# Value projections in quarters, a third slot of lag, and weights laid out before the launch

## The chip, the cores and the metric

The kernel runs on one core of a Trainium2 chip. The metric is the device time of the whole program in microseconds, the median of several runs. The engines are TensorE (PE; its weight loads are listed as PEld), VectorE (DVE), ScalarE (ACT), GpSimd (POOL) and SyncE (SP), which issues most DMAs. They run their own instruction streams in order and wait for one another on semaphores.

## What is computed

One decoder layer for 16 sequences of 128 tokens with 256 features, with layer norms in front of its three parts:

```python
x = x + attn(layernorm(x))            # 16 heads of 64, fixed-point rounding
x = x + xattn(layernorm(x), ctx)      # ctx: (16, 128, 128), 16 heads of 64
x = x + ffn(layernorm(x))             # d_ff 1024, two of 8 experts by LoRA of rank 16

# attn
q, k, v = make_fxp(x @ w_qkv.T)       # clip to +-8, truncate to 1/4096
dots = make_fxp(q @ k.T * 64 ** -0.5)
attn = make_fxp(softmax(dots))
out = make_fxp(attn @ v)
out = make_fxp(out @ w_proj.T + b_proj)

# xattn: the same without make_fxp; k and v from ctx
# ffn: sum over 2 experts of top_v[k] * relu(h @ wi.T + (h @ A.T) @ B.T) @ wo.T
```

All tensors are float32. The kernel reaches that precision on TensorE with operands split into a high part (type F32R) and a low part: every large product is three matmuls, low x high, high x low, high x high (`split3`, lines 405 to 407).

## The kernel before

The 16 sequences form G = 4 groups of 4, 512 tokens each. The kernel runs self-attention for the four groups, then cross-attention for the four, then the feed-forward for the four. The functions of these stages are named a_, b_ and c_. The x tile stays in SBUF throughout.

In an attention stage a group has eight slots, one for each pair of heads. A slot s of self-attention issues on TensorE, in this order (`a_slot`, line 505): the q block and the k block of pair s (6 matmuls of 512 columns each, `a_block`); the transposes of the softmax weights of slot s-2 (`a_transpose`); the output projection of slot s-3 (`project_out`, 12 matmuls of 256 columns); the product of weights and values of slot s-2 (`a_attend`); in slots 0 to 3 alone, two value blocks of 512 columns, each for one sequence and half of the heads; and the scores of slot s (`a_scores`). The lag of two slots gives the softmax time: ScalarE takes signs (the rounding to fixed point needs them) and exponentials, VectorE converts to int16 and clips, and takes the reciprocal of the sums, GpSimd multiplies the exponentials by it (`a_weights`, tile p_int). There is one buffer each of e_sb, p_int and rsum. VectorE's order in a slot is q and k conversions and clips, work of the layer norm of the next group or the previous group's output, reciprocal, output of slot s-2 (`a_out`: oi, oT_hi, oT_lo), the value conversions and clips, and the conversion of the scores. `y_out` (two additions of the bias) comes in slot 2 and reads what the projection of all eight slots has summed up. `normed_T` transposes the next group's normalised rows in slot 7; ScalarE and VectorE make xnT_hi and xnT_lo of them.

A cross-attention slot (`b_slot`, line 614) is built alike. Its q, k and v blocks all go through one PSUM bank, `one_ps`: q is copied out by ScalarE, v and k by VectorE (`b_v_rows`, `b_k_rows`), and the next block waits for that copy. VectorE's order is: row maxima of the scores, copies of the transposed weights (aT_sb), value copy, k copy, reciprocal, second value copy, oT_lo, norm work.

The weights come from HBM as the reference has them. TensorE transposes those of self-attention before and during group 0 (`a_weights_T`), ScalarE makes the high part, VectorE the low part. Those of cross-attention need no transposes: GpSimd's queue loads the high part, SP's the float32 values in pieces to raw_b, and GpSimd subtracts (six pieces of 1,024 columns, line 351). TensorE also transposes ctx, 4 matmuls in each group, and all weights of the feed-forward between the last cross-attention scores and the first up block (`c_weights`, 13 pieces), where the last two lagged slots of cross-attention are finished as well.

The loads on SP's queue stand in this order: a first part of w_qkv, x of group 0, the rest of w_qkv, w_proj, x of groups 1 to 3, the biases. VectorE waits in slot 1 of group 0 for b_proj and for x of groups 1 to 3 (line 1095 and 1096), then scales bias_a.

Of the kernel before, what the change touches and what calls it, by code (L numbers as in the profile page):

```python
# [25 lines left out]
NF = F // P  # L47
FIX = 4096.0
# [20 lines left out]
def block_index(s):  # L69

    return 4 * s if s < 4 else 16 + 2 * (s - 4)


BLOCKS = block_index(8)


def build(nc, x, ctx, w_qkv, w_proj, b_proj, Wq, Wk, Wv, Wo, bo, wi_w, wo_w, lora_As, lora_Bs,
          top_i, top_v, out):
# [8 lines left out]
    wqkvT_hi = sb("wqkvT_hi", [P, KD, 3 * E], F32R)  # L87
    wqkvT_lo = sb("wqkvT_lo", [P, KD, 3 * E], F32R)
    wpT_hi = sb("wpT_hi", [P, NP, D], F32R)
    wpT_lo = sb("wpT_lo", [P, NP, D], F32R)  # L90
    region_b = mem["at"]
    wq_hi = sb("wq_hi", [P, KD, E], F32R)
    wq_lo = sb("wq_lo", [P, KD, E], F32R)
    wk_hi = sb("wk_hi", [P, E], F32R)
    wk_lo = sb("wk_lo", [P, E], F32R)
    wv_hi = sb("wv_hi", [P, E], F32R)
    wv_lo = sb("wv_lo", [P, E], F32R)
    wo_hi = sb("wo_hi", [P, NP, D], F32R)
    wo_lo = sb("wo_lo", [P, NP, D], F32R)
    wqkv_raw, _, nxt = place("wqkv_raw", [P, 3 * NP, D], F32, at=region_b)  # L100
    wp_raw, _, nxt = place("wp_raw", [P, KD, E], F32, at=nxt)
# [7 lines left out]
    e_sb = sb("e_sb", [P, 8, NT], F32)  # L109
    p_int = sb("p_int", [P, 8, NT], I16)  # L110
# [20 lines left out]
    rsum = sb("rsum", [P, 8], F32)  # L131
    rsc = sb("rsc", [P, 8], F32)
# [3 lines left out]
    growth = sb("growth", [P, 8], F32)  # L136
    top_sb = sb("top_sb", [P, 2], F32)


    ctx_sb, _, nxt = place("ctx_sb", [P, GB, CTX], F32, at=region_a)  # L140
    cT_hi, _, nxt = place("cT_hi", [P, TOK], F32R, at=nxt)
    cT_lo, _, nxt = place("cT_lo", [P, TOK], F32R, at=nxt)
    p_f, _, nxt = place("p_f", [P, 8, NT], F32, at=nxt)
    wi_raw, _, nxt = place("wi_raw", [P, NF, D], F32, at=nxt)
    wd_raw, _, nxt = place("wd_raw", [P, KD, F], F32, at=nxt)
    lb_raw, _, nxt = place("lb_raw", [P, NF, 2, RANK], F32, at=nxt)
    lb1, _, nxt = place("lb1", [P, NF, 3, 2, RANK], F32, at=nxt)
# [36 lines left out]
    def sem(name):  # L184
        return nc.alloc_semaphore(name)

    ld_x0, ld_xr, ld_wq, ld_wk, ld_wv, ld_wp, ld_b = (
        sem(n) for n in ("ld_x0", "ld_xr", "ld_wq", "ld_wk", "ld_wv", "ld_wp", "ld_b"))
    ld_wq2, out_done = sem("ld_wq2"), sem("out_done")
    ld_raw, ld_bhi, ld_bb = sem("ld_raw"), sem("ld_bhi"), sem("ld_bb")  # L190
    ld_ctx, ld_cw, ld_idx, ld_top = sem("ld_ctx"), sem("ld_cw"), sem("ld_idx"), sem("ld_top")
    wb_lo, g_tick = sem("wb_lo"), sem("g_tick")

# [54 lines left out]
    with nc.Block() as block:  # L248
# [43 lines left out]
        def _(pool):  # L292
# [34 lines left out]
            def a_slot(g, s, first=False):  # L327
# [4 lines left out]
                if s == 2:  # L332
                    inv_std(g + 1)
# [1004 lines left out]
```

## Time and profile before

| | |
|---|---|
| median of 3 runs | 730.95 us (729.81 to 731.84) |
| the profiled execution | span 730.2 us, 15,676 instructions |
| TensorE busy | 672.8 us (92%) |
| VectorE busy | 550.0 us (75%) |
| ScalarE busy | 413.7 us (57%) |
| GpSimd busy | 272.6 us (37%) |
| HBM read and written | 16.16 MB, 2.10 MB |
| GB/s in the first of 40 slices (18.25 us) | 312 |

Busy times are unions over the engine's instructions. Matmuls overlap in the records, since each is listed with its pipeline's length: the distance from one start to the next is the time that one takes on TensorE when they follow each other. In a timeline a row's columns are start us, us, engine, line, operation, out<-in, shapes and count; a bracket behind it is the idle time of the engine before it, and what ended it. A row of windows gives the stretch and its length, the busy us and the instructions of PE, PEld, DVE, ACT and POOL, then the granted TensorE clock (1.00 is 2.4 GHz, 0.50 is 1.2 GHz), the DMA engines' share and GB/s. The profiled execution is one run of its own, 0.8 us below the median of the timed ones.

### The profile page before, as it was taken

Reading aid. Unit: us, or ns where it says so; the run is one execution under the profiler, and the core shown is the slowest. Engines: PE = TensorE matmul, PEld = TensorE weight load, DVE = VectorE, ACT = ScalarE, POOL = GpSimd, SP = SyncE. Lnnn points to the kernel's source line nnn. Section 1 sums busy time; section 2 is a strip of 40 time slices with the busy share of each in tenths; the row PEclk is TensorE's granted clock in tenths of the full one; section 3 lists DMA queues with packets and bytes.
Section 4 is the critical chain, followed back from the end, with each engine's and each line's share of the span. In section 5 each row is a group of like instructions: output and inputs, shape, how many; then the busy total and the mean of one; then the engine's idle time right before and its main releaser. Section 6 shows DMA issues by size and latency. Waiting matters only on the chain.

```text
span 730.2 us, 15676 instructions
## 1 busy us (share of the span) xinstructions
PE 672.8 (92%) x5186; PEld 551.7 (76%) x5186; DVE 550.0 (75%) x1142; ACT 413.7 (57%) x1443; POOL 272.6 (37%) x610
## 2 busy tenths in 40 slices
PE   5998879989998899878989999999999889999997
PEld 4777768777886788766777877787788777888986
DVE  5879887887888789757767776677667668787775
ACT  4677756767776777764455455445544563433432
POOL 1166754454445534535354344234333532010110
PEclk9999999999999999999999999999999999999999
DMA  9135100000000000050000000000000000000000
GB/s 312 49 111 150 60 30 1 1 1 1 0 0 0 0 0 0 0 153 1 1 2 16 1 1 1 14 0 0 0 0 0 0 1 1 2 30 0 29 29 29
DMA packets 17002, 18.75 MB, mean 26 GB/s; under 512 B 2851, under 2 KB 15427, under 8 KB 16963
## 3 DMA queue, kind: packets, MB, share of 16 engines
q1 hardware_dynamic: 15330, 15.11, 6.4%
q0 software_dynamic: 1632, 3.15, 1.5%
q8 instruction: 21, 0.34, 0.2%
q14 instruction: 19, 0.15, 0.1%
HBM read 16.16 MB, written 2.10 MB: 25 GB/s over the span
## 4 chain that ended last, share of the span: by engine, by line
PE 35%; POOL 7%; DVE 6%; ACT 3%; issue 3%; DVEq 0%; POOLq 0%; ACTq 0%
PE bank L405 9%; PE bank L407 8%; PE bank L406 8%; POOL p_f L363 6%; PE bank L583 3%; ACT e_sb L889 2%; PE bank L595 2%; PE bank L607 1%; DVE mx L1164 1%; PE bank L729 1%; PE bank L741 1%; DVE bn_st L966 1%; DVE oT_lo L1206 1%; POOL p_int L316 0%; DVE v_sb L1137 0%
## 5 line engine op out<-in xcount | busy, mean ns | idle before, releaser
L363 POOL TENSOR_SCALAR p_f<-e_sb,rsum 128x128 f32<-128x128 f32 x256 | 95.6, 398 | 156.7 <-DVE rsum L1199 156.7
L316 POOL TENSOR_SCALAR p_int<-e_sb,rsc 128x128 int16<-128x128 f32 x256 | 116.2, 475 | 6.3 <-issue 5.7
L889 ACT ACTIVATE e_sb<-bank,neg_max 128x128 f32<-128x128 f32 x256 | 90.1, 380 | 12.1 <-DVE neg_max L1168 11.9
L804 ACT ACTIVATE sgn<-bank 128x512 bf16<-128x512 f32 x96 | 57.2, 598 | 57.6 <-PE bank L407 57.6
L819 ACT ACTIVATE e_sb<-si 128x128 f32<-128x128 int16 x256 | 75.1, 303 | 0.0
L1021 DVE SCALAR_TENSOR_TENSOR ri<-sgn,bank 128x512 int16<-128x512 bf16 x96 | 62.5, 677 | 7.3 <-ACT sgn L804 6.5
L875 ACT COPY q_sb<-bank 128x512 f32<-128x512 f32 x32 | 18.8, 587 | 84.5 <-PE bank L407 84.5
L311 POOL TENSOR_TENSOR rsc<-rsum,growth 128x8 f32<-128x8 f32 x32 | 6.7, 209 | 156.0 <-DVE rsum L1047 156.0
L889 ACT ACTIVATION_READ_ACCUMULATOR e_sb<-bank,neg_max 128x1 f32 x256 | 55.9, 218 | 0.0
L405 PE MATMUL bank<-xnT_hi,wqkvT_lo 128*128 128x512 f32 x128 | 53.6, 419 | 2.2 <-DVE ri L1021 1.3
L1175 DVE COPY aT_sb<-bank 128x512 f32<-128x512 f32 x64 | 41.2, 685 | 12.7 <-PE bank L583 12.5
L407 PE MATMUL bank<-xnT_hi,wqkvT_hi 128*128 128x512 f32 x128 | 50.2, 392 | 0.0
L406 PE MATMUL bank<-xnT_lo,wqkvT_hi 128*128 128x512 f32 x128 | 49.9, 390 | 0.0
L819 ACT ACTIVATION_READ_ACCUMULATOR e_sb<-si 128x1 f32 x256 | 49.9, 195 | 0.0
L809 ACT ACTIVATE aT_sb<-bank 128x1024 f32<-128x1024 int16 x32 | 32.8, 1026 | 25.6 <-PE bank L464 25.6
L1145 DVE COPY k_sb<-bank 128x512 f32<-128x512 f32 x32 | 22.1, 691 | 30.0 <-PE bank L407 30.0
L583 PE MATMUL bank<-ident,p_f 128*128 128x128 f32 x256 | 34.1, 276 | 11.3 <-POOL p_f L363 10.5
L583 PEld LDWEIGHTS bank<-ident,p_f 128*128 128x128 f32 x256 | 28.5, 140 | 20.1 <-POOL p_f L363 15.4
L950 ACT CAST oT_hi<-hid 128x512 fp32r<-128x512 f32 x32 | 19.9, 622 | 41.0 <-DVE hid L1282 41.0
L1164 DVE TENSOR_REDUCE mx<-bank 128x4 f32<-128x512 f32 x64 | 40.8, 677 | 0.4
L464 PE MATMUL bank<-ident_b,p_int 128*128 128x128 bf16 x256 | 19.8, 220 | 22.7 <-POOL p_int L316 22.7
L405 PE MATMUL bank<-wpT_hi,oT_lo 128*128 128x256 f32 x128 | 39.1, 305 | 1.8 <-DVE oT_lo L1042 1.8
(162 smaller groups left out, 2039.5 us busy)
## 6 DMA issues: line engine op xcount, KB each, us to landing
x_sb<-in_x SPq DMA_DIRECT2D x4, 512.0 KB, 10.3
wqkv_raw<-in_L_attn_w_qkv SPq DMA_DIRECT2D x2, 1024.0 KB, 10.2
out<-x_sb SPq DMA_DIRECT2D x8, 256.0 KB, 2.2
wqkv_raw<-in_L_attn_w_qkv SPq DMA_DIRECT2D x2, 512.0 KB, 5.1
wp_raw<-in_L_attn_w_proj SPq DMA_DIRECT2D x1, 1024.0 KB, 12.3
raw_b<-in_L_xattn_Wq SPq DMA_DIRECT2D x2, 512.0 KB, 3.3
wq_hi<-in_L_xattn_Wq POOLq DMA_DIRECT2D x2, 512.0 KB, 4.1
wo_hi<-in_L_xattn_Wo POOLq DMA_DIRECT2D x2, 512.0 KB, 8.4
```

The lines of the kernel that those rows point to most:

```text
L316: i = nc.gpsimd.tensor_scalar(p_int[:, t, :], e_sb[:, t, :], rsc[:, t:t + 1], -0.5, ALU.mult, ALU.add)
L363: i = nc.gpsimd.tensor_scalar(p_f[:, t, :], e_sb[:, t, :], rsum[:, t:t + 1], 0.0, ALU.mult, ALU.add)
L405: pe.matmul(out_, wl, mh, start=first, stop=False, **kw)
L406: pe.matmul(out_, wh, ml, start=False, stop=False, **kw)
L407: return pe.matmul(out_, wh, mh, start=False, stop=last, **kw)
L583: last = pe.transpose(pT_ps[hh][:, b * P:(b + 1) * P], p_f[:, GB * hh + b, :], ident[:, :])
L804: nc.scalar.activation(sgn[:, m % 2, :], proj_ps[m % 2][:, :], ACT.Sign).then_inc(a_sgn, 1)
L819: last = nc.scalar.activation(e_sb[:, t, :], si[:, i, j * P:(j + 1) * P], ACT.Exp, scale=1.0 / FIX, accum_out=sums[:, t:t + 1])
L889: last = nc.scalar.activation(e_sb[:, t, :], s_ps[hh][:, (t % 4) * P:(t % 4 + 1) * P], ACT.Exp, bias=neg_max[:, t:t + 1], scale=DH ** -0.5 ...
L1021: V.scalar_tensor_tensor(ri[:, i, :], sgn[:, i, :], -0.5, proj_ps[i][:, :], ALU.mult, ALU.add).then_inc(a_ri, 1)
L1164: V.reduce_max(mx[:, half], s_ps[hh][:, :].rearrange("p (a t) -> p a t", a=GB), AX).then_inc(b_mx, 1)
L1175: i = V.tensor_copy(aT_sb[:, GB * hh:GB * hh + GB, :].rearrange("p a t -> p (a t)"), pT_ps[hh][:, :])
```

## The change

- Values: each slot of both attention stages projects a quarter of the heads' value columns (256) for two sequences, 12 matmuls of 256 columns in self-attention and 6 in cross-attention, in place of two blocks of 512 columns in slots 0 to 3.
- The lag of transposes and attend is three slots, that of the projection four. e_sb, p_int, p_f, rsum and rsc have two buffers. `y_out` moves to slot 3.
- Self-attention: the output projection and the transposes come first, then the values, then attend; `normed_T` comes behind attend. oT_hi is made by ScalarE.
- Cross-attention: q, transposes, value quarter, half of the projection, k, the other half, attend, scores.
- Weights and ctx arrive transposed, in the order in which they are used. No weight goes through TensorE any more. GpSimd's queue loads all high parts, SP's and ScalarE's queues the float32 values, and GpSimd subtracts: in self-attention 14 pieces of 512 columns in front of and during group 0's slots 0 to 3, for cross-attention six pieces of 1,024 columns in slots 3 and 6 of groups 1 to 3, for the feed-forward during cross-attention's group 0. Block 0 of q, k and v is split by ScalarE and VectorE.
- x of group 0 is loaded first, in four parts on two queues. x of groups 1 to 3 comes behind all self-attention weights. VectorE waits for it in slot 1 as before. 14 matmuls on a zeroed tile run before the data are there.

```diff
+BLOCKS = 3 * NP
+LAG = 3
...
-    e_sb = sb("e_sb", [P, 8, NT], F32)
-    p_int = sb("p_int", [P, 8, NT], I16)
+    e_sb = sb("e_sb", [P, 2, 8, NT], F32)
+    p_int = sb("p_int", [P, 2, 8, NT], I16)
...
+            def a_rows(g, s):
+                m = 3 * s + 2
+                a_block_free(g, m)
+                for i in range(2):
+                    b = 2 * (s % 2) + i
+                    for kt in range(KD):
+                        last = split3(proj_ps[m % 2][:, i * QW:(i + 1) * QW],
+                                      [t[:, kt, b * P:(b + 1) * P] for t in (xnT_hi, xnT_lo)],
+                                      [w[:, s // 2, kt, :] for w in (wv_hi, wv_lo)], i == 0 and kt == 0, kt == KD - 1,
+                                      skip_group_check=True)
+                last.then_inc(a_blk, 1)
...
+                for i in range(2):
+                    a_block(g, 3 * s + i, [w[:, s, :, i, :] for w in (wqk_hi, wqk_lo)])
+                lagged = not (first and s < LAG)
+                if lagged:
+                    a_transpose(n - LAG, (s - LAG) % 2)
+                if not (first and s <= LAG):
+                    p = (s - LAG - 1) % NP
+                    if first:
+                        wait(pe, w_lo, low_count("p", p // 2))
+                    project_out(n - LAG - 1, p, a_olo, a_pj, (wp_hi, wp_lo), (a_z, 2 * g))
...
+                a_rows(g, s)
+                if lagged:
+                    p = (s - LAG) % NP
+                    gg = g if s >= LAG else g - 1
+                    a_attend(n - LAG, p, BLOCKS * gg + 6 * (p // 2) + 6)
                 if s == NP - 1:
-
                     normed_T(g + 1, lambda: wait(pe, a_ri, BLOCKS * (g + 1)))
...
                 else:
                     b_block(g, s, "q")
                     transposes()
-                    if s < 4:
-                        b_block(g, s, "v", 0)
-                    project()
+                    b_block(g, s, "v")
+                    project((0, 1))
                     b_block(g, s, "k")
-                    attend()
...
+                    project((2, 3))
...
+                attend()
+                b_scores(g, n, s)
...
+                    for loaded in ld_x[1:]:
+                        dve.wait_ge(loaded, 16)
```

## Rows read from the trace of the kernel before

**Rows 1.** Busy times in windows: self-attention groups 0 to 2, cross-attention 0 and 1, hand-over
```profile
17.90:89.40 71.50, 64.56 (x508) 52.51 (x508) 60.18 (x121) 49.68 (x171) 37.80 (x66) 1.00 0.32 95
89.40:168.30 78.90, 71.30 (x570) 57.98 (x568) 63.53 (x135) 53.96 (x187) 37.31 (x77) 0.98 0.03 9
168.30:243.00 74.70, 69.76 (x570) 56.72 (x568) 60.97 (x135) 53.74 (x187) 35.00 (x76) 1.00 0.00 0
317.70:390.70 73.00, 64.77 (x526) 51.06 (x524) 50.23 (x107) 36.89 (x152) 35.61 (x86) 0.98 0.07 19
390.70:456.90 66.20, 63.51 (x527) 51.20 (x525) 46.09 (x100) 34.03 (x147) 25.36 (x68) 1.00 0.02 5
588.90:609.10 20.20, 16.33 (x141) 14.16 (x140) 13.60 (x27) 11.11 (x34) 3.61 (x11) 1.00 0.01 2
```

**Rows 2.** Timeline of TensorE, a self-attention slot with values, and a weight load
```profile
18.00 0.19 PEld L406 LDWEIGHTS bank<-xnT_lo,wqkvT_hi 128*128 128x128 f32 x1
...
189.97 0.50 PE L405 MATMUL bank<-xnT_hi,wqkvT_lo 128*128 128x512 f32 x1
...
192.83 0.62 PE L464 MATMUL bank<-ident_b,p_int 128*128 128x128 bf16 x8
...
194.86 1.09 PE L475 MATMUL bank<-aT_sb,v_sb 128*64 128x128 f32 x16
195.89 0.50 PE L405 MATMUL bank<-wqkvT_hi,xnT_lo 128*128 128x512 f32 x1
...
198.87 1.16 PE L498 MATMUL bank<-k_sb,q_sb 64*128 64x128 f32 x16
200.01 0.50 PE L405 MATMUL bank<-xnT_hi,wqkvT_lo 128*128 128x512 f32 x1
```

**Rows 3.** Timeline of TensorE, the transposes of a self-attention slot without values
```profile
154.95 0.62 PE L464 MATMUL bank<-ident_b,p_int 128*128 128x128 bf16 x8 [1.18 <-POOL p_int L316]
```

**Rows 4.** Timelines of VectorE and GpSimd in self-attention
```profile
194.60 0.42 DVE L1025 TENSOR_SCALAR k_sb<-ri 128x512 f32<-128x512 int16 x1
...
201.17 1.27 DVE L1056 TENSOR_TENSOR raw_b<-bank,bias_a 128x512 f32<-128x512 f32 x2
...
101.45 2.32 DVE L1025 TENSOR_SCALAR v_sb<-ri 128x512 f32<-128x512 int16 x2
...
100.76 2.39 POOL L351 TENSOR_TENSOR wo_lo<-raw_b,wo_hi 128x1024 fp32r<-128x1024 f32 x1 [4.78 <-DMA raw_b<-in_L_xattn_Wo]
```

**Rows 5.** Timeline of TensorE, a cross-attention slot with values
```profile
400.93 0.50 PE L405 MATMUL bank<-xnT_hi,wq_lo 128*128 128x512 f32 x1
...
403.25 0.50 PE L405 MATMUL bank<-wv_hi,cT_lo 128*128 128x512 f32 x1
...
404.05 0.28 PE L405 MATMUL bank<-wo_hi,oT_lo 128*128 128x256 f32 x1
...
405.49 0.44 PE L405 MATMUL bank<-cT_hi,wk_lo 128*128 128x512 f32 x1
...
409.33 0.50 PE L405 MATMUL bank<-xnT_hi,wq_lo 128*128 128x512 f32 x1
```

**Rows 6.** Timeline of VectorE in the same slot
```profile
403.49 1.29 DVE L1175 COPY aT_sb<-bank 128x512 f32<-128x512 f32 x2 [0.86 <-PE bank L583]
404.69 0.68 DVE L1137 COPY v_sb<-bank 128x512 f32<-128x512 f32 x1
```

**Rows 7.** Timeline of the head, and the window 12 to 18 us
```profile
5.84 1.40 DVE L966 BATCH_NORM_STATS2 bn_st<-x_sb 128x6 f32<-128x256 f32 x4 [5.84 <-DMA x_sb<-in_x]
...
9.26 1.38 DVE L985 TENSOR_SCALAR xn<-x_sb,mv,rstd 128x256 f32<-128x256 f32 x4 [1.59 <-POOL rstd L306]
...
14.78 1.52 PE L438 MATMUL bank<-ident,xn 128*128 128x128 f32 x8
...
12.00:18.00 6.00, 5.25 (x31) 5.04 (x30) 5.37 (x9) 4.45 (x8) 0.00 (x0) 1.00 1.07 374
```

**Rows 8.** Timeline of TensorE, group 1, slot 1
```profile
106.70 0.62 PE L464 MATMUL bank<-ident_b,p_int 128*128 128x128 bf16 x8 [2.69 <-POOL p_int L316]
```

More of the change, by code:

```diff
@@ L47 @@
 NF = F // P
+NQ = 4
+QW = E // NQ
 FIX = 4096.0
@@ L66, in sbuf_map, with build @@
     return place, state
[L69 to L78, printed above, removed]
+BLOCKS = 3 * NP
+LAG = 3
+def build(nc, x, ctxT, wqk, wv, wp, b_proj, wB, bo, wiT, wdT, lora_AT, lora_BT, top_i, top_v, out):
     place, mem = sbuf_map(nc)
@@ L615, in b_slot @@
                 n = NP * g + s
-                lag2 = not (first and s < 2) and not (drain and s >= 2)
-                if s == 0 and not drain:
-                    wait(pe, ld_ctx, 16 * (g + 1))
-                    wait(pe, ln_lo, 2 * (G + g) + 1)
-                    for b in range(GB):
-                        last = pe.transpose(one_ps[:, b * P:(b + 1) * P], ctx_sb[:, b, :], ident[:, :])
-                    last.then_inc(b_cT, 1)
+                lagged = not (first and s < LAG) and not (drain and s >= LAG)
@@ L729, in up @@
                     pe.matmul(u[:, :], lb1T[:, s * P:(s + 1) * P], lowT[:, :], start=False, stop=True).then_inc(c_u, 1)
-                if first and s == 2:
-                    wait(pe, cw_lo, len(C_PREP))
                 if not drain and s > 0:
@@ L1079, in between_groups @@
                 if not first:
-                    for slot, j, part in ((3, 0, 0), (4, 0, 1), (6, 1, 0), (7, 1, 1)):
+                    for slot, j, part in ((4, 0, 0), (5, 0, 1), (6, 1, 0), (7, 1, 1)):
                         if s == slot:
@@ L1087, in a_slot @@
                 n = NP * g + s
-                base = block_index(s)
+                lagged = not (first and s < LAG)
                 if s == 2:
@@ L1101, in a_slot @@
                 if not (first and s == 0):
-                    a_recip(n - 1)
-                if not (first and s < 2):
-                    a_out(n - 2)
-                if s < 4:
-                    if s == 0 and not first:
-                        wait(dve, a_av, NP * g - 4)
-                    if s == 2:
-                        wait(dve, a_av, NP * g)
-                    fix_blocks(g, base + 2, [v_sb[:, j % 4, 512 * (j // 4):512 * (j // 4) + 512]
-                                             for j in (2 * s, 2 * s + 1)], (1.0, 1.0))
-                if s == 2 and not first:
+                    a_recip(n - 1, (s - 1) % 2)
+                if lagged:
+                    a_out_low(n - LAG)
+                if s == LAG and not first:
                     y_out(g)
@@ L1148, in b_slot @@
                 n = NP * g + s
-                lag2 = not (first and s < 2) and not (drain and s >= 2)
+                lagged = not (first and s < LAG) and not (drain and s >= LAG)
                 if not drain:
@@ L1156, in b_slot @@
                 if first:
-                    for slot, j, part in ((3, 0, 0), (4, 0, 1), (5, 1, 0), (6, 1, 1)):
+                    for slot, j, part in ((4, 0, 0), (5, 0, 1), (6, 1, 0), (7, 1, 1)):
                         if s == slot:
```

856 lines of the change are left out of this document (421 added, 435 removed).

## The prediction

> **What bounds the kernel now.** I read the page first: TensorE is busy 92% of the span, so time can come only from its idle time, from work taken off it, or from the head, before it is fed. Then I cut the span by group, each cut where TensorE has issued the last scores of a group [rows 1]. The self-attention groups 2 and 3 take 74.7 us each, group 1 takes 78.9, a cross-attention group 66.2, the stretch between cross-attention and the feed-forward 20.2. In a self-attention group VectorE is busy 61.0 of 74.7 us and ScalarE 53.7: neither is the bound on average.
>
> Then one slot on TensorE. A slot with two value blocks is gapless: q and k 2.86, transposes and output projection 2.03, attend 1.03, two value blocks 2.98, scores 1.14, together 10.04 [rows 2]. The slots without values (four of eight) have only 7.06 us of such work, and there TensorE waits 1.18 us at the transposes for GpSimd's softmax weights [rows 3]. Counting 4 x 10.04 + 4 x 7.06 + 0.88 for the transposes of the next group's rows gives 69.3 of 74.7: 5.4 us of idle per group.
>
> A cross-attention slot with two value blocks takes 8.40: q and transposes 2.32, value 0.80, projection 1.44 (12 matmuls of 256 columns, 0.12 apart), then k, attend, value, scores 3.84 [rows 5]. It too has no gap, but barely: k may start only when VectorE has copied the value block out of the one shared bank, and that copy runs behind the two copies of the transposed weights, from 404.69 to 405.37, while k starts at 405.49 [rows 5, 6].
>
> **Self-attention slots.** The values' columns stay the same in number, 12 matmuls of 256 in each slot for 6 of 512 per block in half of them. With the 0.12 spacing of the projection, a value quarter costs 12 x 0.12 + 0.11 = 1.55 (half of 2.98 is 1.49). Each slot is then 2.86 + 2.03 + 1.55 + 1.03 + 1.14 = 8.6. The bounds: 1.49 if the form costs nothing, and 12 x 0.19 = 2.3 if each weight load showed [rows 2] (a rival, below). The wait of [rows 3] goes: with a lag of three, weights of one slot are needed almost two slots later, against 4.4 us of GpSimd per slot (35.0 in eight, [rows 1]). What is late next is VectorE. After the slot's start k is clipped by 5.0 us [rows 2, 4], scores are wanted at 7.5: covered by 2.5. Moving oT_hi takes a conversion like that of k_sb, 0.42 [rows 4], from VectorE and gives it to ScalarE, whose mean is 6.7 per slot; both fit under 8.6. The rest has no cover at two places: the two bias additions of y_out, 1.28 us [rows 4], stand in front of the score conversions, and the value quarter waits for the q conversion, with some 0.5 us of slack, so 0.8 is lost once a group. At the turn, the transposes (now behind the attend) wait 0.5 for the last conversion, cost 0.88, and the two xnT_lo operations, each about as long as one of y_out's, leave TensorE idle for 0.6. A group is 7 x 8.6 + 0.8 + 10.6 = 71.6.
>
> GpSimd's weight splits now lie beside VectorE. In the trace such a split of 1,024 columns takes 2.39, and two clips that take 0.4 each took 2.32 while it ran [rows 4]. Six of them move into groups 1 to 3. The bounds for one are 0 and 1.5. VectorE is idle for 14 of the 74.7 us of a group [rows 1] and most of its operations have slack, so I take 0.2 each, 1.2 in all, and 0.1 for each of the nine small ones (512 columns) of group 0. The Trainium skill ("SBUF — State Buffer", Reading the diagram) says that GpSimd and a VectorE operation in a fast mode, or with two SBUF inputs, exclude each other for a whole instruction. The row agrees. By that rule alone all six would cost up to 1.5, and the sum would be some 8 us higher.
>
> Groups 1 to 3: 228.3 becomes 3 x 71.6 + 1.2 = 216.0, so -12.3. The 4.2 us by which group 1 is longer than its twins are within this: there GpSimd was late behind a split that waited for a DMA, TensorE idled 2.69, and the granted clock of the group fell to 0.98 [rows 1, 8]. The lag covers that.
>
> **The head.** The weights' transposes go, and the first block waits for the rows alone. x arrived at 5.84, the norm was done at 10.64, from the transposes of xn at 14.78 to the first block at 17.9 are 3.1 [rows 1, 7]. That is 7.9 us behind the arrival of x. x is now in front of the weights, in four parts from two queues; 0.5 MB less ahead of it at 374 GB/s are 1.4 us, so it arrives near 4: first block at 11.9 (11 to 14), -6.0.
>
> **Group 0.** Slots 0 to 2 have no lagged work, 5.6 us on TensorE, but scores wait for the clip at 5.0: 5.0 + 1.14 = 6.2. So 3 x 6.2 + 7.0 (no projection yet) + 3 x 8.6 + 10.6 = 62.0. Against this: VectorE waits in slot 1 for all of x, 11.9 + 6.2 + 5.0 = 23.1 us into the span. Loads for x now stand behind 4.2 MB of weights, and GpSimd's queue loads the high parts from HBM again (3.7 MB). Some 9.3 to 10.1 MB are to land first; at 374 GB/s [rows 7] these end at 26.5 to 28.5. TensorE's next k block waits for VectorE's value conversion: 4.7 us. The bounds are 0 and 10 (the rate of the first slice of the page, 312 GB/s). So long an idle time has been followed by half clock here [rows 8]; 1.0. Group 0: 62.0 + 4.7 + 1.0 + 0.9 = 68.6 against 71.5, -2.9.
>
> **Cross-attention slots.** Work on TensorE: 8.40 less two value blocks (0.80, 0.89) plus a quarter of 0.82 and a split projection: 7.5. But now only half of the projection, 0.72, lies between value and k. From the start of the value block to the end of its copy are 2.12 (403.25 to 405.37, [rows 5, 6]), since the aT_sb copies go first; quarter and half projection cover 1.54. So k waits 0.6 in every slot: 8.15. In a plain slot the row maxima leave some 0.7 of slack before the aT_sb copies. At the end of slot 3 y_out (1.3) and the statistics (half a group's, 0.7) stand before the maxima and the moments (0.4) before the value copy: slot 4 loses 1.6 more. In front of slot 6 two row additions' and applications' 1.4 do: 0.7; slot 0 is 7.85 (its transposes come first) and slot 7 9.1. Sum 7.85 + 4 x 8.15 + 9.8 + 8.85 + 9.1 = 68.2, where 66.2 is now: +2.0 for each of three groups, +6.0. The bounds of a group are 61 (no wait) and 71 (each wait twice as long). The first group's surplus of 6.8 over the others (hand-over, half clock) I lower to 5.0, because ctx needs no transposes: 73.2, +0.2.
>
> **To the feed-forward.** The window of 20.2 has 16.3 us of TensorE work in 141 matmuls. 50 of them are transposes of weights; at 0.10 each (eight in the 2.32 above, [rows 5]) 5.2. The extra lag adds a slot's transposes, projection and attend, 3.3. That gives 18.3 with today's 3.9 us of waits and 14.4 with none. Half of the waits stood behind weight transposes: 16.5, -3.7. From the first up block on nothing changes but the addresses.
>
> **Sum.** -6.0 - 2.9 - 12.3 + 0.2 + 6.0 - 3.7 = -18.7: the profiled execution of 730.2 would be 711.5. The median of the three timed runs is 730.95, 0.8 above it: 712.3.
>
> **Rivals.** (1) Cross-attention does not stall: VectorE reaches the value copy early. Then its groups take 61.0 + 0.9 = 62, 25 us less in four groups: 687. The 405.37 against 405.49 speaks against it. 0.10. (2) Loads of x are in time and the splits hide: -5.7 and -2.1: 704.5. For it: the SP queue may be served before GpSimd's. 0.18. (3) Self-attention is held by its chain, not by TensorE: ScalarE and VectorE wait in turn for each other (sign, conversion, exponentials), and a split that blocks VectorE at its full 1.5 pushes the q conversion over its slack. Six such and half a us in each of 20 slots are 18, less what is counted: +13 or so, 725. The shared-port rule above leads here. 0.15. (4) Slower: the value quarter hangs on the weight load. 576 matmuls of 256 columns are new (12 in 32 slots, 6 in 32); each has its own load, and a load lasts 0.19 [rows 2]. At 0.19 apart for 0.12 they cost 576 x 0.07 = 40, so 752. It decides from 0.153 apart, where the 18.7 are used up. Against it: the projection has the same form with a load each and keeps 0.12. 0.04. My forecast has 0.45; 0.08 is left for what no row shows, such as a late ctx at the hand-over.
>
> **Numbers.** The range reaches from the lower edge of the forecast with (2), 698, to (3), 726: it leaves out (1), (4) and part of the rest. A measurement of this kernel can tell about 0.3%, 2.2 us, from no change. Faster: forecast, (1), (2), (3) and some of the rest, 0.91; same 0.02; slower (4) and some of the rest, 0.07.
>
> **What would show it.** First block near 12. No wait for p_int at the bf16 transposes, and scores 8.6 apart in self-attention, with longer distances at slots 4 and 7. bias_a idle before it for a DMA of x. In cross-attention wk_lo's first matmul idle 0.6 for the copy into v_sb, and distances of 8.15. Value matmuls 0.12 apart. Wrong would make it: cross-attention slots at 7.5, a stall for x over 8, or 256-column value matmuls over 0.13 apart.

## The result, and the profile after

The change makes the kernel slightly slower: 736.89 us median against 730.62, ratio 1.0067 with a 95% interval of 1.0042 to 1.0091. 736.89 is the median of all seven executions, while the ratio leaves out the two slow ones (744.4 us, granted clock 0.963); the other five lie between 732.8 and 738.3. The forecast of 712.3 was 24.6 too low, the sign was wrong, and the time lies outside the range. The profiled execution of the changed kernel has a span of 734.7 us.

The windows of the changed kernel, cut like those of [rows 1] where TensorE has issued the last scores of a group: self-attention groups 0, 1 and 2, cross-attention groups 0, 1 and 2, and the hand-over.

```profile
16.55:87.00 70.45, 63.83 (x496) 53.65 (x496) 49.62 (x106) 46.99 (x162) 40.92 (x75) 0.92 0.46 170
87.00:164.30 77.30, 71.70 (x612) 61.90 (x614) 62.65 (x127) 57.52 (x197) 36.76 (x78) 0.96 0.01 2
164.30:239.20 74.90, 69.64 (x624) 59.95 (x622) 62.92 (x127) 57.33 (x196) 38.13 (x79) 1.00 0.00 0
...
314.00:390.70 76.70, 64.27 (x545) 53.65 (x546) 50.42 (x103) 40.99 (x163) 51.07 (x102) 0.98 0.16 54
390.70:461.00 70.30, 64.81 (x545) 55.16 (x546) 45.86 (x100) 33.80 (x148) 30.46 (x72) 0.98 0.02 5
461.00:529.70 68.70, 63.20 (x545) 53.80 (x546) 45.72 (x100) 33.87 (x148) 24.72 (x66) 1.00 0.01 4
...
598.40:613.80 15.40, 13.78 (x126) 11.89 (x126) 8.03 (x16) 5.13 (x20) 2.80 (x8) 1.00 0.00 1
```

Self-attention should have gained 12.3 us in groups 1 to 3 and gained 1.3; the granted clock of its groups 0 and 1 is 0.92 and 0.96, and that of the first two groups of cross-attention 0.98. Set against the forecast, stage by stage (spans of the profiled executions):

| stage | before | forecast | after |
|---|---|---|---|
| head and self-attention group 0 | 89.4 | 80.5 | 87.0 |
| self-attention groups 1 to 3 | 228.3 | 216.0 | 227.0 |
| cross-attention group 0 | 73.0 | 73.2 | 76.7 |
| cross-attention groups 1 to 3 | 198.2 | 204.2 | 207.7 |
| hand-over and feed-forward | 141.3 | 137.6 | 136.3 |
| span | 730.2 | 711.5 | 734.7 |

**Self-attention.** TensorE's timeline of group 2. The scores rows (k_sb,q_sb) mark the slots: a slot's length is the distance from the scores of the slot before to its own.

```profile
189.00 1.16 PE L547 MATMUL bank<-k_sb,q_sb 64*128 64x128 f32 x16
197.46 1.16 PE L547 MATMUL bank<-k_sb,q_sb 64*128 64x128 f32 x16
...
206.46 0.39 PE L464 MATMUL bank<-wv_hi,xnT_lo 128*128 128x256 f32 x1 [2.80 <-DVE ri L994]
209.10 1.16 PE L547 MATMUL bank<-k_sb,q_sb 64*128 64x128 f32 x16
...
236.93 1.09 PE L479 MATMUL bank<-ident,xn 128*128 128x128 f32 x8 [2.38 <-DVE ri L994]
```

Plain slots are 8.46 apart, a little better than the 8.6 of the forecast, and no transpose waits for p_int any more: the third slot of lag does what it was expected to do. But slot 4 takes 11.64 (197.46 to 209.10), and slot 7 takes 11.93. Both wait for VectorE's ri, the conversion of a projected block. VectorE and GpSimd at these two places (a split is GpSimd's subtraction that makes the low part of a weight piece, here wB_lo):

```profile
200.56 1.28 DVE L1038 TENSOR_TENSOR raw_b<-bank,bias_a 128x512 f32<-128x512 f32 x2
201.76 1.27 DVE L1096 SCALAR_TENSOR_TENSOR si<-s_sgn,bank 128x512 int16<-128x512 bf16 x2
202.95 2.86 DVE L1100 TENSOR_SCALAR si<-si 128x512 int16<-128x512 int16 x2
...
232.28 1.51 DVE L999 TENSOR_SCALAR k_sb<-ri 128x512 f32<-128x512 int16 x1
233.71 2.57 DVE L1053 TENSOR_SCALAR raw_b<-zi 128x512 f32<-128x512 int16 x1
```

```profile
203.28 2.37 POOL L348 TENSOR_TENSOR wB_lo<-wB_raw,wB_hi  x1
...
231.99 1.51 POOL L336 TENSOR_TENSOR x_sb<-x_sb,raw_b 128x512 f32 x1
233.47 2.53 POOL L348 TENSOR_TENSOR wB_lo<-wB_raw,wB_hi  x1
```

The clips of si, 0.51 for two elsewhere in the group, take 2.86: they end at 205.81, just behind the split's end at 205.65. In slot 7 k_sb, 0.41 elsewhere, is held until GpSimd's row addition ends (233.50) and raw_b, also 0.41 alone, until the split does (236.00). Both then stand in front of the conversion that TensorE waits for.

**Head and group 0.** ScalarE, VectorE and TensorE at the head, then VectorE and TensorE at slot 2's start, and three windows: the stretch at half clock (granted clock 0.50), and the time up to the landing of x in two parts:

```profile
10.33 0.62 ACT L793 CAST wqk_hi<-wqk_raw 128x512 fp32r<-128x512 f32 x1 [6.43 <-DMA wqk_raw<-in_wqk]
10.98 0.69 DVE L980 TENSOR_TENSOR wqk_lo<-wqk_raw,wqk_hi 128x512 fp32r<-128x512 f32 x1 [5.42 <-ACT wqk_hi L793]
11.59 1.38 DVE L968 TENSOR_SCALAR xn<-x_sb,mv,rstd 128x256 f32<-128x256 f32 x4
16.55 0.77 PE L464 MATMUL bank<-xnT_hi,wqk_lo 128*128 128x512 f32 x1 [1.49 <-DVE xnT_lo L988]
...
34.29 0.29 DVE L1078 TENSOR_SCALAR bias_a<-bias_a 128x256 f32<-128x256 f32 x1 [3.66 <-DMA x_sb<-in_x]
36.54 0.50 PE L464 MATMUL bank<-xnT_hi,wqk_lo 128*128 128x512 f32 x1 [3.10 <-DVE ri L994]
...
10.67:20.91 10.24, 6.30 (x18) 5.04 (x19) 4.79 (x10) 2.57 (x5) 7.85 (x8) 0.50 1.10 388
...
0.00:18.40 18.40, 9.91 (x27) 5.01 (x28) 5.99 (x17) 3.59 (x5) 11.73 (x25) 0.79 0.90 291
18.40:34.20 15.80, 13.14 (x83) 10.39 (x81) 7.89 (x14) 8.56 (x27) 7.95 (x9) 0.92 1.04 364
```

The statistics were done at 5.6, but in VectorE's queue the low part of the first weight block stands ahead of xn and waits for a load and a cast. The first block starts at 16.55, forecast 11.9, before 17.9. The 14 matmuls on zeros had ended at 7.42; TensorE then idled for 5.69, and from 10.67 to 20.91 the granted clock is 0.50, so most of the first block runs at half clock (its 512-column matmuls are 0.43 apart, 0.24 at full clock). In the kernel before, the matmuls of the first block, from 17.93 on, are 0.23 apart. The wait for x is there: VectorE idles 3.66 (forecast 4.7). x landed at 34.2, where 26.5 to 28.5 was forecast: 291 GB/s were moved in the first 18.4 us and 364 after it, not 374 throughout, and together these are 11.1 MB, not 9.3 to 10.1.

**Cross-attention.** A plain slot of group 2: value quarter, half a projection, then k.

```profile
471.21 0.38 PE L464 MATMUL bank<-wB_hi,cT_lo 128*128 128x256 f32 x1
...
472.62 0.28 PE L466 MATMUL bank<-wB_hi,oT_hi 128*128 128x256 f32 x1
473.38 0.50 PE L464 MATMUL bank<-cT_hi,wB_lo 128*128 128x512 f32 x1 [0.48 <-DVE v_sb L1117]
...
476.01 1.16 PE L648 MATMUL bank<-k_sb,q_sb 64*128 64x128 f32 x16
```

k waits for VectorE's copy of v, as forecast: it starts 0.76 behind the last matmul of the half projection, where 0.12 is the distance without a wait, so 0.64 for the 0.6 of the forecast. The slots are 8.23 apart (forecast 8.15), slot 4 is 9.68 (forecast 9.8).

### The profile page after: what moved, and what is told of

Read it like the earlier page. It is cut to its first block, busy times and chain, and to the rows that moved or that the text cites. A ratio compares the mean times of both kernels' runs of the same rounds, so it can differ in the third digit from the quotient of the medians.

```text
span 734.7 us, 16172 instructions
## 1 busy us (share of the span) xinstructions
PE 667.4 (91%) x5358; PEld 567.3 (77%) x5358; DVE 531.4 (72%) x1080; ACT 413.5 (56%) x1445; POOL 308.7 (42%) x656
## 4 chain that ended last, share of the span: by engine, by line
PE 67%; DVE 16%; issue 8%; ACT 4%; SPq 3%; DMA 2%; DVEq 1%; ACTq 0%
PE bank L464 17%; PE bank L465 14%; PE bank L466 14%; PE bank L636 5%; PE bank L524 4%; PE bank L547 3%; PE bank L648 3%; DVE v_sb L1117 3%; PE bank L624 2%; DVE mx L1144 2%; DVE aT_sb L1155 2%; DMA x_sb<-in_x 2%; PE bank L513 2%; SPq L230 2%; PE bank L479 1%
## 5 line engine op out<-in xcount | busy, mean ns | idle before, releaser
L327 POOL TENSOR_SCALAR p_int<-e_sb,rsc 128x128 int16<-128x128 f32 x256 | 108.1, 440 | 6.3 <-issue 5.9
L464 PE MATMUL bank<-xnT_hi,wqk_lo 128*128 128x512 f32 x128 | 55.1, 430 | 5.5 <-DVE ri L994 3.1
L1185 DVE TENSOR_TENSOR oT_lo<-bank,oT_hi 128x512 fp32r<-128x512 f32 x32 | 22.1, 692 | 43.2 <-ACT oT_hi L905 43.2
L905 ACT CAST oT_hi<-bank 128x512 fp32r<-128x512 f32 x32 | 18.8, 587 | 59.3 <-PE bank L636 59.3
L466 PE MATMUL bank<-xnT_hi,wqk_hi 128*128 128x512 f32 x128 | 51.1, 399 | 0.0
L465 PE MATMUL bank<-xnT_lo,wqk_hi 128*128 128x512 f32 x128 | 50.6, 395 | 0.0
L464 PE MATMUL bank<-wv_hi,xnT_lo 128*128 128x256 f32 x128 | 37.5, 293 | 9.9 <-DVE ri L994 9.9
L1096 DVE SCALAR_TENSOR_TENSOR si<-s_sgn,bank 128x512 int16<-128x512 bf16 x64 | 40.8, 679 | 1.5 <-ACT s_sgn L853 1.5
L464 PE MATMUL bank<-wp_hi,oT_lo 128*128 128x256 f32 x128 | 38.7, 303 | 2.2 <-DVE oT_lo L1025 2.2
## 6 DMA issues: line engine op xcount, KB each, us to landing
wB_hi<-in_wB POOLq DMA_DIRECT2D x1, 3072.0 KB, 11.6
x_sb<-in_x SPq DMA_DIRECT2D x3, 512.0 KB, 20.9
```

Of the source, the lines that this page charges most:

```text
L327: i = nc.gpsimd.tensor_scalar(p_int[:, half, t, :], e_sb[:, half, t, :], rsc[:, half, t:t + 1], -0.5, ALU.mult, ALU.add)
L464: pe.matmul(out_, wl, mh, start=first, stop=False, **kw)
L465: pe.matmul(out_, wh, ml, start=False, stop=False, **kw)
L466: return pe.matmul(out_, wh, mh, start=False, stop=last, **kw)
L1096: V.scalar_tensor_tensor(si[:, i, :], s_sgn[:, i, :], -0.5, s_ps[i][:, :], ALU.mult, ALU.add).then_inc(a_si, 1)
```

## The experiments

Distances between slots are read from the scores rows of TensorE's timeline, as above. The kernel before ran beside each set (runs 1 to 4, 5 to 8, 9 to 12): 730.73, 729.94 and 730.14 us. The ratios are to it; the changed kernel's own is 1.0067.

**1. Splits left out.**

```diff
-            sp.dma_start(wB_raw[:, :, :], wB).then_inc(ld_wB, 16)
...
+                    nc.gpsimd.dma_start(wB_lo[:, :, :], wB).then_inc(ld_wB, 16)
...
-                    raw, hi, lo = (w[:, bass.ds(chunk, 1), :].rearrange("p a e -> p (a e)") for w in (wB_raw, wB_hi, wB_lo))
+                    hi, lo = (w[:, bass.ds(chunk, 1), 0:1].rearrange("p a e -> p (a e)") for w in (wB_hi, wB_lo))
...
```

> Leaves out nearly all of the low-part work on wo's weights: the six GpSimd subtractions of groups 1 to 3 (2.37 us each) touch one column, and the low copy is loaded from memory by GpSimd's queue in place of the raw one. Theory (the splits hold VectorE in full in slots 3 and 6, where it has no slack): slots 4 and 7 of groups 1 to 3 come down from 11.6 and 11.9 us to about 8.5 and 10.0, some 4.5 to 5 us per group, so about 14 us less in all, near 723. Rival (VectorE's own work of these slots, y_out's two additions, the fixed-point passes and the row additions, is what makes them late; the split lies in VectorE's slack): the slots stay at 11.6 and 11.9 to within 0.5 each, and the time stays within 3 us of 737. The prediction's own size was 0.2 per split, 1.2 in all.

This kernel leaves the low part of these weights unmade, so it shows the price of the splits and is not a usable version.

Measured: 720.55 us, ratio 0.9868 [0.9816, 0.9920]. In groups 1 to 3 slot 4 is 9.50 and slot 7 is 9.94, where the changed kernel has 11.64 and 11.93; plain slots stay at 8.46. A split costs 2.14 and 1.99 at its two places: 4.1 per group, 12.4 in three, in place of 1.2. The rival falls as the main cause. Slot 4 doesn't come down to the 8.5 that I expected, though: 1.04 above a plain slot stays without any split, for y_out, which the forecast had put at 0.8. It is the splits on top of that which it had missed.

**2. Splits in 24 pieces, one in each slot.**

```diff
-                if not first and s in (3, 6):
+                if not first:
+                    piece = 8 * (g - 1) + s
...
-            pe.wait_ge(wB_done, 6)
+            pe.wait_ge(wB_done, 24)
```

> The same split work in 24 pieces of 256 columns, one at the end of GpSimd's work in every slot of groups 1 to 3, in place of six of 1024. Theory (what costs is one long hold at a place without slack): a piece of about 0.6 us is taken up by VectorE's slack in the plain slots and costs 0.6 at most in slots 4 and 7, so groups 1 to 3 come down from about 75 us to 71 or 72, near 726 in all. Rival (held time adds up wherever it lies, since the slot is set by VectorE's chain): the groups stay at 75 and the plain slots grow from 8.46 to about 9.0.

Measured: 729.26, ratio 0.9979 [0.9962, 0.9996]. Slot 4 is 10.03 and slot 7 is 10.31, plain slots 8.46: the pieces cost 0.53 and 0.37 there and nothing elsewhere. The total is worse than that, because TensorE waited 7.27 us for the last piece, queued behind GpSimd's work of slot 7, before it could enter cross-attention (its slot 0 took 18.06, otherwise 10.6; the granted clock was 0.50 for 10.24 us from within that wait). My expectation had not seen that.

**3. Whole projection between v and k.**

```diff
                     b_block(g, s, "v")
-                    project((0, 1))
+                    project()
                     b_block(g, s, "k")
-                    project((2, 3))
```

> In cross-attention the output projection runs whole between the value and the key quarters, instead of half in front and half behind the key quarter. Theory (k waits for VectorE's copy of v out of the one buffer, 2.8 us in the median in the waits, and half the projection doesn't cover it): the slots of 8.23 us come down by 0.4 to 0.7, 28 of them, so 11 to 18 us less, 719 to 726. Rival (the slot's length is TensorE's busy time and the wait moves to the next one, the exponentials or the reciprocal): no change, within 2 us of 737.

Measured: 717.43, ratio 0.9820 [0.9801, 0.9839]. Two scores rows of group 2 in the timeline of TensorE:

```profile
462.20 1.16 PE L648 MATMUL bank<-k_sb,q_sb 64*128 64x128 f32 x16
469.71 1.16 PE L648 MATMUL bank<-k_sb,q_sb 64*128 64x128 f32 x16
```

7.51 in place of 8.23, and k starts without idle time; slot 4 is 8.95 in place of 9.68. An undisturbed group goes from 68.7 to 64.4 and group 0 from 76.7 to 73.4. That is 16.2 us in the four groups, within what was expected. The medians differ by 19.5; the other 3 are not shown to be an effect of this edit. In its profiled execution x landed at 32.5 instead of 34.2, and slot 7 of self-attention's group 0 begins its scores at 82.9 instead of 85.8; but with the same loads in the same order x landed anywhere from 31.8 (run 6) to 35.3 (run 5).

**4. x of group 1 before the projection's weights.**

```diff
+                if (kind, i) == ("p", 0):
+                    sp.dma_start(bias_a[:, :], b_proj.partition_broadcast(P)).then_inc(ld_b, 16)
+                    load_x(1)
...
-                    for loaded in ld_x[1:]:
-                        dve.wait_ge(loaded, 16)
+                    dve.wait_ge(ld_x[1], 16)
...
+            for loaded in ld_x[2:]:
+                dve.wait_ge(loaded, 16)
```

> The bias and the x rows of group 1 are loaded ahead of the projection's weights, and VectorE waits in slot 1 for these alone and for the other x rows only behind group 0. Theory (VectorE's 3.66 us wait for x in slot 1 holds TensorE for 3.10 us, and the half clock behind it costs about 1): slot 2 begins at 39 instead of 42.2 and the time falls by 3 to 4 us, near 733. Rival (the weights of the blocks behind, now loaded later, stop TensorE as long): slot 2 earlier, but slots 3 to 7 of group 0 longer by the same 3 us, no change. The prediction had put this wait at 4.7.

Measured: 734.80, ratio 1.0068 [1.0042, 1.0094]: no different from the changed kernel. The place did what was expected and more: bias_a has no wait, slot 2's scores are at 36.8 (42.2 after the change), slot 7's at 80.5 (85.8). Its profiled execution, 727.98 at a mean granted clock of 0.988, shows it; others of its six runs took 733.17 at 0.981 and 738.36 at 0.969. The times of this program go with the clock, and at a like clock they are lower than those of the changed kernel: 734.26 and 735.34 at 0.976 here, 736.5 and 736.9 at 0.979 and 738.28 at 0.974 there. That speaks for a gain of 2 to 3 us, given back by a lower clock in most runs; at which place, and why it is lower, their records don't show.

**5. Norm before the first low part.**

```diff
-            dve.wait_ge(w0_hi, 1)
-            raw, hi, lo = low_part("qk", 0)
-            V.tensor_tensor(lo, raw, hi.bitcast(F32), ALU.subtract).then_inc(w0_lo, 1)
             norm_apply(0, 0, (ln_T, 0))
             ...
+            dve.wait_ge(w0_hi, 1)
+            ...
```

> At the head, VectorE applies the norm to x (xn) and copies the identity before it makes the low part of the first weight block, instead of behind it. Theory (rstd is there at 7.5 us, but the low part waits for ScalarE's cast of a block that lands at 9.7 to 10.3, and xn stands behind it in the queue): xn at 7.5 to 8.9, the transposes at 9 instead of 12 to 13, and then the first matmul with the low weights waits for the low part, ready at about 11 plus its 0.7, so the first scores come about 3 us earlier (21 instead of 24) and the time falls by 2 to 3. Rival (the loads of the later weight blocks and of x set the pace of group 0): the first scores come earlier, but slot 7 of group 0 still starts near 82 to 86 and the time falls by less than 1.

Measured: 737.12, ratio 1.0106 [1.0062, 1.0150]. The timeline of VectorE, and of TensorE in slot 2:

```profile
7.51 1.38 DVE L968 TENSOR_SCALAR xn<-x_sb,mv,rstd 128x256 f32<-128x256 f32 x4 [1.93 <-POOL rstd L314]
...
35.28 0.29 DVE L1078 TENSOR_SCALAR bias_a<-bias_a 128x256 f32<-128x256 f32 x1 [6.49 <-DMA x_sb<-in_x]
...
37.53 0.79 PE L464 MATMUL bank<-xnT_hi,wqk_lo 128*128 128x512 f32 x1 [5.93 <-DVE ri L994]
```

xn comes 4 us earlier, the first block starts at 12.65 instead of 16.55, and the first scores are at 21.4 instead of 24.5. x lands no earlier (35.3, after the change 34.2), so the wait for it grows from 3.66 to 6.49, and slot 7 starts at 86.9. The rival was right: alone, this gains nothing.

**6. Pieces where VectorE has slack.**

```diff
-                if not first and s in (3, 6):
-                    chunk = 2 * (g - 1) + (s - 3) // 3
+                if not first:
+                    for piece in {0: (0, 1), 1: (2, 3), 2: (4,), 4: (5,), 5: (6, 7)}.get(s, ()):
...
```

> The splits of groups 1 to 3 in pieces of 256 columns as in the earlier run, but put into slots 0, 0, 1, 1, 2, 4, 5, 5 of a group: none in slots 3, 6 and 7, whose ends VectorE sets. Theory: slot 4 falls to the 9.50 us and slot 7 to the 9.94 of the run without splits, plain slots stay at 8.46, a group is 71.3; and TensorE no longer waits 7.3 us at the entrance of cross-attention for the last piece; about 722 to 724 in all. Rival (two pieces in one slot, 1.4 us of hold, are more than its slack): slots 1, 2 or 5 grow by up to 0.7 each, a group is 72.5 or more.

Measured: 721.00, ratio 0.9896 [0.9834, 0.9958]. TensorE's and VectorE's timeline around slot 4 of group 2:

```profile
188.36 1.16 PE L549 MATMUL bank<-k_sb,q_sb 64*128 64x128 f32 x16
195.20 0.39 PE L466 MATMUL bank<-wv_hi,xnT_lo 128*128 128x256 f32 x1 [0.65 <-DVE ri L996]
197.86 1.16 PE L549 MATMUL bank<-k_sb,q_sb 64*128 64x128 f32 x16
```

```profile
193.85 0.70 DVE L1102 TENSOR_SCALAR si<-si 128x512 int16<-128x512 int16 x2
```

The clips of si take 0.70 (0.72 at this place in run 1, without a split), the idle time before the values is 0.65 instead of 2.80, slot 4 is 9.49 and slot 7 is 9.94, with all of the split work done. So the price from run 1 holds when the work is done. Groups 1 to 3 take 212.1 together, the changed kernel's 227.0.

**7. The feed-forward's splits in pieces, in cross-attention's group 0.**

```diff
-                if s in (1, 2):
+                for piece in {1: (0, 1), 2: (2, 3), 3: (4, 5), 4: (6,), 5: (7,)}.get(s, ()):
...
+                for piece in {4: (0,), 5: (1,), 6: (2, 3, 4), 7: (5, 6, 7)}.get(s, ()):
```

> The four splits of the feed-forward's weights (2.37 us each) that stand in slots 1 to 4 of cross-attention's group 0 become 16 pieces of about 0.6 to 0.7 us in slots 1 to 7. Theory (a split holds VectorE's maxima and through them the copy of v, 2.46 and 2.84 us of TensorE's idle time in slots 2 to 4): slots 3 and 4 fall from 11.8 and 10.6 to about 9.7, slots 5 to 7 grow by at most 0.3 each, group 0 falls from 76.7 to about 74, the time by 2 to 3. Rival (these slots wait for y_out and the copy of v, the splits being hidden): group 0 stays at 76 to 77.

Measured: 736.42, ratio 1.0081 [1.0057, 1.0106]. Group 0 takes 73.5 in place of 76.7, as expected, but the total doesn't move: in this profiled execution slots of self-attention were stretched instead (slot 4 of group 3 took 13.77, with half clock for 6.83 us). Nor are the 3.2 us of group 0 the price of the splits alone. The profile of run 6, whose splits there are untouched, has 74.2 for the same group: its slots 3 and 4 are 10.3 and 9.7, where the changed kernel's profile has 11.8 and 10.6. Slot 3's 1.5 is half clock (0.50 from 348.6 to 352.0). Slot 4's 1.0 is a hold: a split that starts at 355.42 holds neg_max for 1.4, while in run 6 both neg_max were through, in 0.28, as that split started. So one and the same schedule gives 74.2 or 76.7, and against the first the pieces are worth some 0.7. The changed kernel's timelines of VectorE, group 0, slots 2 and 4, and of GpSimd in slot 2:

```profile
343.22 1.27 DVE L1144 TENSOR_REDUCE mx<-bank 128x4 f32<-128x512 f32 x2
344.42 1.56 DVE L1148 TENSOR_SCALAR neg_max<-mx 128x4 f32<-128x4 f32 x2
...
356.43 1.45 DVE L1148 TENSOR_SCALAR neg_max<-mx 128x4 f32<-128x4 f32 x2
```

```profile
343.50 2.37 POOL L403 TENSOR_TENSOR wi_lo<-wi_raw,wi_hi 128x1024 fp32r<-128x1024 f32 x1
```

The two maxima, read from a PSUM bank, keep their 1.27 beside the split. The two neg_max, 0.28 elsewhere, end only behind it. My expectation had the maxima held; it is neg_max.

**8. All of 3 to 7.** The edits above together.

> All in one: pieces of the splits in the slots with slack in both stages, the whole projection between v and k, norm before the first low part, x of group 1 before the projection's weights. If the parts add up: 736.9 less 12.5 (splits of groups 1 to 3), 19.5 (projection), 2 to 3 (head), 3 (x), 2 to 3 (splits of cross-attention's group 0), so about 697, and surely under 705. Rival (they share their cover: what the projection hides in group 0 is what the splits held, and the half clock comes back at another place): 700 to 708.

Measured: 697.41, ratio 0.9566 [0.9537, 0.9596]; the parts add up, and the rival falls. Of the head's 3 us, lost when alone, most is kept here, since x no longer comes late: against run 4 the first scores are at 20.9 instead of 24.1 and slot 7 of group 0 at 78.1 instead of 80.5.

**9. Splits whole, but in slots 1 and 5.**

```diff
-                if not first and s in (3, 6):
-                    chunk = 2 * (g - 1) + (s - 3) // 3
+                if not first and s in (1, 5):
+                    chunk = 2 * (g - 1) + (s - 1) // 4
```

> The changed kernel with the six splits left whole (1024 columns, 2.37 us each) but moved from slots 3 and 6 to slots 1 and 5 of groups 1 to 3. Theory (the place decides, since VectorE sets the ends of slots 4 and 7 alone): slots 4 and 7 fall to 9.5 and 9.9 to 10, the slots behind the moved splits (2 and 6) grow by at most 0.5 each, a group is 71.3 to 72.3 and the time 722 to 726. Rival (the size decides, a hold of 2.37 us is longer than the slack of any slot): slots 2 and 6 grow by 1.5 to 2 each, a group stays at 74 to 75, time 733 to 737. In pieces of 256 columns at the same places the group was 71.3.

Measured: 722.97, ratio 0.9913 [0.9889, 0.9937]. The timelines of VectorE and GpSimd:

```profile
178.71 2.66 DVE L999 TENSOR_SCALAR q_sb<-ri 128x512 f32<-128x512 int16 x1
178.69 2.39 POOL L348 TENSOR_TENSOR wB_lo<-wB_raw,wB_hi  x1
```

VectorE is held as long as before: q_sb takes 2.66 for 0.41. But the slots behind grow by only 0.65 and 0.52 (expected 0.5 at most), slot 7 by 0.2, and slot 4 is back at 9.49: 1.4 per group for holds of the same length that cost 4.1 in slots 3 and 6. The place decides most of it, the size some 1.4.

**10. The output projection behind the values (in self-attention, on the version of run 8).**

```diff
-                    project_out(n - LAG - 1, p, a_olo, a_pj, (wp_hi, wp_lo), (a_z, 2 * g))
...
                 a_rows(g, s)
+                    project_out(n - LAG - 1, p, a_olo, a_pj, (wp_hi, wp_lo), (a_z, 2 * g))
```

> The best version so far (697.4) with one part of the change undone: in self-attention the output projection stands behind the values again, not in front. Theory (the value block waits for VectorE's conversion of k, which ends about 1.4 us behind the transposes' start, and the projection's 1.4 us of matmuls cover that): TensorE waits 0.8 to 1.4 us in front of the values in all slots, 32 of them, so 26 to 45 us more, about 725 to 740. Rival (the transposes alone cover it, or ScalarE and VectorE take the matmuls of the projection as slack elsewhere): under 5 us more, near 700.

Measured: 727.75, ratio 0.9969 [0.9952, 0.9987], 30.3 us above run 8. TensorE's timeline:

```profile
180.68 1.16 PE L552 MATMUL bank<-k_sb,q_sb 64*128 64x128 f32 x16
186.21 0.39 PE L469 MATMUL bank<-wv_hi,xnT_lo 128*128 128x256 f32 x1 [0.94 <-DVE ri L998]
190.30 1.16 PE L552 MATMUL bank<-k_sb,q_sb 64*128 64x128 f32 x16
```

Plain slots are 9.55 to 9.61 for 8.46, with the wait for VectorE's conversion in front of the values. This part of the change earns its place.

**11. A lag of two slots (on the version of run 8).**

```diff
-LAG = 3
+LAG = 2
```

> The best version so far (697.4) with the lag put back from three slots to two in both attention stages; the double buffers stay. Theory (in a plain self-attention slot GpSimd ends p_int about 2.1 us behind the place where the transposes of two slots back would stand, so TensorE waits for it in every slot): self-attention's slots of 8.46 become 9.8 to 11, 32 slots, 45 to 80 us more, 740 to 780. Rival (with two buffers the softmax chain keeps up by itself, and the lag brought nothing): 697 to 705.

Measured: 784.41, ratio 1.0754 [1.0729, 1.0779], 87.0 above run 8. TensorE's timeline:

```profile
215.70 1.16 PE L552 MATMUL bank<-k_sb,q_sb 64*128 64x128 f32 x16
221.62 0.62 PE L518 MATMUL bank<-ident_b,p_int 128*128 128x128 bf16 x8 [1.79 <-POOL p_int L329]
226.11 1.16 PE L552 MATMUL bank<-k_sb,q_sb 64*128 64x128 f32 x16
```

Self-attention's slots become 10.4 to 12.1, with the wait for p_int, and cross-attention's plain slots about 8.0 for 7.5. Self-attention loses 70 us, cross-attention 18: the total is above my upper end, since I had not counted cross-attention. Not all of it is the wait itself: five slots of self-attention's groups 1 to 3 are 1.5 longer than their twins, each with a stretch at half clock, some 8 us together.

**12. The norm's statistics and moments moved, in cross-attention (on the version of run 8).**

```diff
-                if not drain and s in (1, 3):
+                if not drain and s in (1, 2):
...
-                if s == 4 and not drain:
-                    norm_moments()
...
                     b_k_rows(g, s)
+                    if s == 4:
+                        norm_moments()
```

> The best version so far (697.4), and in cross-attention the second half of the norm's statistics in slot 2 instead of slot 3, its moments behind the copies of v and k of slot 4 instead of in front. Theory (TensorE's idle 1.20 us in slot 4 in front of k is VectorE being late with y's two additions, 1.28, the statistics, 0.74, and the moments, 0.37): slot 4 falls from 8.96 by 1.0 to 1.1 in each group, the time by about 4, to 693.5. Rival (the time returns in slots 5 and 6, where the norm's own chain through GpSimd ends later and xn stands): 0 to 2 us less.

Measured: 691.09, ratio 0.9462 [0.9441, 0.9483], the fastest version: 39 us below the kernel before, 45.8 below the changed one. The scores rows of slot 4 of group 2:

```profile
456.71 1.16 PE L653 MATMUL bank<-k_sb,q_sb 64*128 64x128 f32 x16
464.50 1.16 PE L653 MATMUL bank<-k_sb,q_sb 64*128 64x128 f32 x16
```

Slot 4 is 7.79 for 8.95, and slots 5 to 7 keep their 7.5, 8.0 and 9.4. That is 1.16 in each of three groups; in group 0, where run 8's slot 4 had half clock (11.03), it is 7.98. By the distances groups 0 to 3 gain 5.2, the medians 6.3, more than the 4 expected. Its page has TensorE busy for 95% of 690.2 us.

## Why the prediction was wrong, step by step

- **Self-attention slots, right.** 8.46 measured for 8.6. 256-column value matmuls are 0.12 apart, so rival (4) fell. With the splits out of the way, groups 1 to 3 take 212.1 (run 6); the forecast had 214.8 without its splits. Runs 10 and 11 show that both the order and the lag carry this. Of the 11.0 us by which groups 1 to 3 missed, the next two terms are 11.2 and 2.3, and these slots give 2.7 back.
- **GpSimd's splits, the main mis-sized term.** The sum had 0.2 for each of six, 1.2 in all; they cost 12.4 (run 1 or 6 against the changed kernel), 11.2 more. Two sentences failed. "VectorE is idle for 14 of the 74.7 us [...] most of its operations have slack": that is an average, and slots 3 and 6 are the places where y_out, and k_sb with the fixed-point pass, have used the slack up. The forecast had itself charged slots 4 and 7 for lateness of VectorE, so there was none left for a split. And the bound of 1.5, from [rows 4], was no upper bound: there the clips came 0.69 us behind the split's start, so that only the rest of it held them. The same trace has a longer hold, which I did not look up: two xn of 0.41 each take 2.77 when they come 0.12 behind the start of a split, 2.0 more.

```profile
60.73 2.77 DVE L985 TENSOR_SCALAR xn<-x_sb,mv,rstd 128x256 f32<-128x256 f32 x2
```

```profile
60.61 2.42 POOL L351 TENSOR_TENSOR wq_lo<-raw_b,wq_hi 128x1024 fp32r<-128x1024 f32 x1 [3.44 <-DMA wo_hi<-in_L_xattn_Wo]
```

The upper end is the split's own length, 2.37, and run 9 shows that at a place with slack 2.3 of hold costs 0.5 to 0.65. Rival (3) had the mechanism, but with 1.5 as its price for a split; its half a us in each of 20 slots did not come (plain slots are 8.46), and its 725 is still 12 too low. The rule of the Trainium skill ("SBUF — State Buffer", Reading the diagram), that whichever of the two starts first has the ports for its whole instruction and the other is blocked, agrees with these rows: si ends 0.16 behind the split, q_sb in run 9 0.29. It should have set the bound.

- **Half clock, left out but for 1.0.** In group 1 of self-attention slot 4 took 13.0 and slot 7 12.8, where groups 2 and 3 have 11.6 and 11.9: 2.3 more, granted clock 0.96. In cross-attention slot 3 of group 0 cost 1.5 more in the same way, slots 4 and 5 of group 1 1.6. Each such stretch, 3.41 us long, lies behind 1.9 to 2.8 us of TensorE's idle time. But idle times of 2.81 and 2.38 us in group 1, which half clock followed, recur as 2.80 and 2.38 in group 2, where none did. Windows of 8 us from the start of the longer one, in group 1 and in group 2:

```profile
126.00:134.00 8.00, 5.19 (x42) 4.43 (x42) 6.69 (x11) 2.56 (x11) 2.38 (x2) 0.79 0.00 0
203.30:211.30 8.00, 5.20 (x52) 4.39 (x52) 7.80 (x14) 3.96 (x19) 2.36 (x3) 1.00 0.00 0
```

A stall's price is thus its length, and at times 1 to 1.5 us more; what decides it, these runs don't show.

- **Head, 4.65 short.** The step "That is 7.9 us behind the arrival of x", measured in the kernel before and carried over to the new order of work, took no account of the new low part queued ahead of xn, nor of the load that it waits for: 5.42 us of VectorE's idle time. Run 5, with the order turned round, has the first block at 12.65, so 3.9 of the 4.65 are this step. It also shows that the head is worth nothing while x is late.
- **Group 0, 1.85 short, and nearer than it deserved.** The wait for x was 3.66, forecast 4.7, but x landed at 34.2 and not by 28.5: the wait was short only because VectorE too was late, which is luck. The step that failed is the 374 GB/s, read from one window of the kernel before and used for the whole time. What made the group longer is that its first slot took 9.0 for 6.2, some 1.9 of it half clock (ten of its matmuls 0.43 apart for 0.24), which the forecast did not have here.
- **Cross-attention, right in kind.** Undisturbed groups take 68.7 (forecast 68.2). The wait for v was read from [rows 5, 6] correctly: in run 3, which covers it, the slots fall to 7.51. Group 0 was put 3.5 too low: half clock 1.5, the splits beside VectorE 1.7 (1.0 in slot 4 and 0.7 that the pieces of run 7 save). Groups 1 to 3 were put 3.5 too low: half clock in group 1 1.6, the slots 1.5, and the rest rounding.
- **To the feed-forward, right.** The hand-over takes 15.4 (forecast 16.5).

The differences by stage are +6.5, +11.0, +3.5, +3.5 and -1.3: the 23.2 between the forecast and the profiled span.

## What to carry to other kernels

Price work on GpSimd by the place at which it holds VectorE: nearly its own length where VectorE's lateness already ends a slot (2.0 to 2.1 of 2.37 here), a quarter of it where VectorE has slack, and nothing that shows where it is also cut up (run 6). When a stage is bound by two engines in turn, look for what can be reordered behind a copy that TensorE waits for (the whole projection, 16 us here; the norm's statistics and moments, 5 to 6 us) before looking for less work. A gain in front of a load that comes late is no gain until the load is moved as well.

## What was not expected of the hardware

A VectorE operation that comes behind the start of a GpSimd subtraction can be held until that ends, however small it is: neg_max on 128x4 took 1.56 for two beside a split of 2.37. Held in these traces were the tensor_scalar operations from SBUF to SBUF: si, q_sb, k_sb, raw_b, xn, neg_max. Operations that read PSUM went on beside a split (the maxima 1.27 for two, the copy of v 0.68), and so did the norm's statistics from SBUF (bn_st, 0.40 at 334.49 beside a split from 334.43 to 336.81). And the same program's time goes with the granted clock: 727.98 us at 0.988 and 738.36 at 0.969 (run 4).
